# Splitting the row maxima on DVE instead of on POOL, in an attention and feed-forward kernel

## Time and profile before

| | |
|---|---|
| three runs | median 218.69 us (218.49 to 219.09) |
| profiled execution | 218.52 us, span 216.7 us |
| PE, matrix products | busy 166.3 us, 77% |
| DVE | 151.9 us, 70%, 287 instructions |
| ACT | 141.2 us, 65%, 286 instructions |
| POOL | 105.1 us, 49%, 275 instructions |
| mean granted clock of PE | 0.952 |

### The profile page before, as it was taken

The page is one execution under the profiler, slowest core; times in us unless marked ns, Lnnn a source line. Parts: engine busy times, 40 slices in busy tenths (PEclk is TensorE's granted clock), DMA queues, the critical chain, the costliest instruction groups (busy, mean ns, idle before and its releaser), DMA issues.

```text
span 216.7 us, 4308 instructions
## 1 busy us (share of the span) xinstructions
PE 166.3 (77%) x1378; PEld 97.9 (45%) x1378; DVE 151.9 (70%) x287; ACT 141.2 (65%) x286; POOL 105.1 (49%) x275
## 2 busy tenths in 40 slices
PE   0008629674969896899899899989989987974963
PEld 0003214332757553475466467556556644523412
DVE  2549906443597976768997998898899796156382
ACT  3220136983657887577888778779688877973531
POOL 4403242419863829772653565284264456345250
PEclk9999999975899999589999999999999999999799
DMA  4945589671112721162025006104300000000000
GB/s 146 321 141 157 149 257 367 255 214 31 28 46 64 207 54 48 49 200 76 0 73 152 27 22 182 51 0 137 113 0 5 0 28 8 20 5 0 27 0 24
DMA packets 15714, 19.95 MB, mean 92 GB/s; under 512 B 2604, under 2 KB 14012, under 8 KB 14684
## 3 DMA queue, kind: packets, MB, share of 16 engines
q1 hardware_dynamic: 11753, 14.94, 23.4%
q10 hardware_dynamic: 3939, 4.74, 6.6%
HBM read 15.20 MB, written 4.19 MB: 90 GB/s over the span
## 4 chain that ended last, share of the span: by engine, by line
PE 38%; POOL 20%; issue 12%; DVE 11%; DMA 9%; ACT 5%; ACTq 1%; SPq 1%; POOLq 0%; DVEq 0%
PE psO L462 9%; PE psA L428 8%; PE psB L446 6%; POOL hw L332 6%; DMA q_stack<-mt 5%; DVE mneg L761 3%; PE psG L564 3%; PE psG L534 2%; PE psG L554 2%; POOL hrms L989 2%; DVE h L851 2%; DMA q_stack<-q_scratch 2%; DMA q_scratch<-q_parts 2%; DVE gu L840 2%; ACT th L682 2%
## 5 line engine op out<-in xcount | busy, mean ns | idle before, releaser
L761 DVE TENSOR_REDUCE mneg<-psA 128x2 f32<-128x512 f32 x128 | 81.8, 678 | 22.1 <-PE psA L428 22.1
L608 ACT ACTIVATE probs<-psB 128x512 f32<-128x512 f32 x128 | 73.2, 597 | 12.3 <-PE psB L446 11.8
L428 PE MATMUL psA<-k_stack,q_stack 72*128 72x256 bf16 x256 | 54.3, 303 | 16.9 <-DMA q_stack<-q_scratch 16.9
L446 PE MATMUL psB<-q_stack,k_stack 75*128 75x256 bf16 x256 | 51.4, 285 | 9.1 <-DMA q_stack<-mt 7.1
L462 PE MATMUL psO<-probs,vt 128*32 128x256 f32 x512 | 37.7, 416 | 1.0 <-ACT probs L608 1.0
L428 PEld LDWEIGHTS psA<-k_stack,q_stack 72*128 72x128 bf16 x256 | 22.9, 104 | 34.0 <-issue 25.5
L332 POOL TENSOR_TENSOR hw<-h,lnw 128x512 f32<-128x512 f32 x15 | 19.1, 1274 | 34.9 <-DVE h L851 26.5
L446 PEld LDWEIGHTS psB<-q_stack,k_stack 75*128 75x128 bf16 x256 | 24.2, 102 | 21.6 <-DMA q_stack<-mt 7.9
L462 PEld LDWEIGHTS psO<-probs,vt 128*32 128x32 f32 x512 | 14.1, 115 | 15.2 <-issue 7.9
L840 DVE SCALAR_TENSOR_TENSOR gu<-th,psG 128x512 f32<-128x512 f32 x15 | 10.3, 687 | 9.3 <-ACT th L682 9.3
L682 ACT ACTIVATE th<-psG,tscale 128x512 f32<-128x512 f32 x15 | 10.3, 688 | 8.0 <-PE psG L534 8.0
(11 more groups left out here) (133 smaller groups left out, 261.6 us busy)
## 6 DMA issues: line engine op xcount, KB each, us to landing
k_stack<-k_scratch SPq DMA_DIRECT2D x21, 192.0 KB
q_stack<-q_scratch SPq DMA_DIRECT2D x21, 192.0 KB
q_scratch<-q_parts SPq DMA_DIRECT2D x24, 64.0 KB, 3.1
k_scratch<-k_parts SPq DMA_DIRECT2D x18, 64.0 KB, 3.0
w_sb<-in_L_ffn_w_gate_dram ACTq DMA_DIRECT2D x1, 1024.0 KB, 7.8
w_sb<-in_L_ffn_w_up_dram ACTq DMA_DIRECT2D x1, 1024.0 KB, 10.8
w_sb<-in_L_ffn_w_down_dram ACTq DMA_DIRECT2D x1, 1024.0 KB, 9.0
out_dram<-y_sb SPq DMA_DIRECT2D x8, 128.0 KB, 1.8
```

The lines of the kernel that those rows point to most:

```text
L428: mm = pe.matmul(psA[n % A_BANKS][:, qt * L:(qt + 1) * L], q_stack[0:STACK, t % NBUF, bh, qt * P:(qt + 1) * P], k_stack[0:STACK, t % NBUF, ...
L446: mm = pe.matmul(psB[b % 2][:, lt * L:(lt + 1) * L], k_stack[:, t % NBUF, bh, lt * P:(lt + 1) * P], q_stack[:, t % NBUF, bh, :], start=Tru ...
L608: act.activation(probs[:, b % RING, :], psB[b % 2][:, :], ACT.Exp, scale=SCALE).then_inc(s_exp, 1)
L761: dve.tensor_reduce(mneg[:, k % MBUF, QT * (bh % HALF):QT * (bh % HALF + 1)], psA[n % A_BANKS][:, :].rearrange("p (q l) -> p q l", q=QT), ...
```

## The change

The four operations of the split leave POOL's list and stand in DVE's, at m = 16 + 16 k: behind the last maximum of the half tile and, where h_max has the same m as that maximum, behind h_max. The waits are the same (all 8 maxima of the half tile, and the transpose two half tiles before, for the buffer). Nothing else moves.

```diff
-POOL_M, POOL_RSTD = 21, 71
+DVE_M, POOL_RSTD = 16, 71
...
                                       negate=True).then_inc(s_red, 1)
+                k = half_at(m, DVE_M)
+                if k is not None:
+                    dve.wait_ge(s_red, HALF * (k + 1))
+                    if k >= 2:
+                        dve.wait_ge(s_mt, k - 1)
+                    worst, part = mneg[:, k % MBUF, :], m_parts[:, k % 2]
+                    link(dve.tensor_copy(part[:, 0, :], worst))
+                    link(dve.tensor_tensor(mrest[:, :], worst, part[:, 0, :], ALU.subtract))
+                    link(dve.tensor_copy(part[:, 1, :], mrest[:, :]))
+                    dve.tensor_tensor(part[:, 2, :], mrest[:, :], part[:, 1, :], ALU.subtract).then_inc(s_ms, 1)
                 if m == DVE_W:
...
-                k = half_at(m, POOL_M)
-                if k is not None:
-                    pool.wait_ge(s_red, HALF * (k + 1))
-                    if k >= 2:
-                        pool.wait_ge(s_mt, k - 1)
-                    worst, part = mneg[:, k % MBUF, :], m_parts[:, k % 2]
-                    link(pool.tensor_copy(part[:, 0, :], worst))
-                    link(pool.tensor_tensor(mrest[:, :], worst, part[:, 0, :], ALU.subtract))
-                    link(pool.tensor_copy(part[:, 1, :], mrest[:, :]))
-                    pool.tensor_tensor(part[:, 2, :], mrest[:, :], part[:, 1, :], ALU.subtract).then_inc(s_ms, 1)
```

## The result

The kernel with the split on DVE takes 225.1 us (median of 4 runs, 224.39 to 225.49) against 218.61 before (218.49 to 219.09): ratio 1.0295, 95% interval 1.0269 to 1.032. It is 6.5 us slower; 216.3 was predicted, in a range up to 218.8. On POOL, behind the place that the split left, the old numbers hold again (L996). A ratio leaves out every execution over 1.5% above the fastest one of its kernel, so where executions scatter it can differ from the quotient of the medians, which are of all of them.

A forecast was written before the change was run, and what follows sets the result against it. PE sets the pace in regular tiles, DVE close behind; late splits stopped PE for 7.8 us. Terms -0.4 - 3.9 + 0.8 - 0.5 + 1.7 - 0.1 = -2.4 us took 218.69 to 216.3, range 213.7 to 218.8.

The forecast's parts named there:

- The first split's transpose: At the start, PE transposes at 23.36 instead of 23.76; the gain of 0.4 us goes into the span.
- A split takes 0.72 us of DVE's list: Cost of four linked steps on DVE: 0.68 us, or 0.8 straight behind a maximum.
- The odd-numbered splits: In regular tiles their 0.8 us fall on DVE's 0.44 + 0.34 of waiting and cost nothing.
- One mark of a wrong forecast: Forecast is wrong if ACT or PE waits over 1 us for POOL between 52 and 58 us.
- 4 x 0.43 = 1.7 us lost: Four even-numbered splits in regular tiles (eighth to fourteenth): L795 ends later, so PE's L511 starts 0.43 us later each.
- rival (c): Sixth split: PE idles about 1.5 instead of 2.11 us, its clock stays up, gain up to 2.2, time 214.1; chance 0.18.
- -3.9: Third split: PE's wait near 48 us goes, the first weight transpose (L497) starts 3.7 to 4.2 us earlier, 3.9 taken.
- +0.8: Fourth split: DVE is packed there and PE waits for its result, so 0.8 us is lost.
- POOL's own queue moves up by what the four steps took: Behind the third split, POOL's rests end 1.1 to 2.0 us earlier, just in time for ACT.
- Rival (b): Third split's gain given back by late rests or second weight matrix: 1.3 of 3.9 us remain, time 218.9; chance 0.14.
- -0.1: Sixth split: h_max still waits for POOL's hw, so L511 starts at 88.2 instead of 88.30, gain 0.1 us.
- Rival (a): DVE's and POOL's steps hold each other up at seven places, 5.9 us together, time 222.2, slower; chance 0.12.

The follow-up runs named there:

- fill4: The changed kernel plus four filler products on PE ahead of the transposes of the sixth, eighth, up to the sixteenth split: 219.91 us, ratio 1.0014 to the kernel before.
- second_split: The kernel before, POOL's splits kept, plus the four operations repeated on DVE behind h_max of the sixth, eighth, up to sixteenth half tile, unread: 226.05 us, ratio 1.0272.
- fourth_on_pool: The kernel of fill4 with the fourth split alone back on POOL: 217.79 us, ratio 0.9849 to the kernel before.
- late_even_on_dve: The kernel before with only the sixth, eighth, up to the sixteenth split on DVE, all others on POOL: 225.37 us, ratio 1.0267.
- fourth_on_dve: The kernel before with the fourth split alone moved to DVE: 221.63 us, ratio 1.0137.
- third_on_dve: The kernel before with the third split alone moved to DVE: 219.02 us (215.26 to 222.09), no ratio.
- third_early_pool: The kernel before, all splits on POOL, the third put ahead of the first weight matrix's rounding in POOL's list: 218.76 us, ratio 0.9922.
- odd_on_pool: The changed kernel with every second split, beginning with the second, back on POOL at its old place: 219.2 us, ratio 0.9898 to the kernel before.

## Why the prediction was wrong

**Right.** The first split's transpose comes 23.76 - 16.93 = 6.83 us behind the first product before and 24.25 - 17.77 = 6.48 after: 0.35 earlier, 0.4 was said; but the first B product gained only 0.1 (7.71 us lie between the two, before 7.47), and the tile grew by 0.38. The third split's wait goes and L497 starts at 51.95 (51.0 to 51.5 was said, in a kernel that began 0.84 earlier). A split takes 0.72 us of DVE's list (0.68). The odd-numbered splits are covered, though DVE's wait of 0.34 still stands there (at 140.20) and only the one of 0.44 is gone. A regular tile whose clock stays up grows by 0.49 (0.43); PE's wait of 0.47 lies one product ahead of where it was put, at pass A for its bank and not at L511. L511 at the sixth split starts at 88.34 (88.2). One mark of a wrong forecast was met as well: ACT waited over 1 us for POOL between 52 and 58 (1.20, at 56.49).

**The step that failed first** is "From L511 to the next tile PE has no gap that would take this back; so 4 x 0.43 = 1.7 us lost". It prices a PE that comes 0.43 us late at the full clock. But the delay is idle time of PE, and with it PE fell to the lower clock in two of the four tiles, for 1.5 us more each. The four tiles cost 5.2 us instead of 1.7. The prediction had seen this effect at the sixth split and used it there alone, as a possible gain in rival (c). fill4 and second_split show it from both sides: with PE kept busy no regular tile falls to the lower clock (none of eight in fill4 and fourth_on_pool), and with only DVE's load added they do (two of four, as with the change; one of four in late_even_on_dve).

**The second is the third split**, "-3.9", with the fourth at "+0.8". The gain was there at 51.95 and mostly gone at 66.27. "POOL's own queue moves up by what the four steps took" is the step that failed: it was to be 1.1 to 2.0 us, and it was nothing (7.88 us in place of 7.73 to the end of the rests), since DVE's clipping now met two of POOL's operations, which grew by 1.07 and 0.98 us. Rival (b) named this mechanism, POOL's queue moving up too little, with 2.6 us; in fact 3.1 of 4.4 us were given back by L511. The fourth split took 2.4 us of DVE's list (57.76 to 60.16) in place of 0.8 in this profile, and the clock was at 0.66 from 57 to 66. Together the stretch from 44.70 to 73.19 gained 1.2 us instead of 3.1.

**The third term**, the sixth split, "-0.1": the tile grew by 1.76. Here too PE waits 1.58 and 0.45 in place of 2.11, and the clock was low in both kernels. How much of the 1.76 belongs to the change stays open: the same tile took 22.06, 22.42 and 24.1 us in fourth_on_dve, third_on_dve and third_early_pool, which change nothing in it, and 24.81 in odd_on_pool, whose sixth split is where it was before (all but the first in executions 2 to 3 us above their medians). late_even_on_dve gives 1.98 for it, at the same uncertainty, and second_split 0.08.

**Rival (a)** said 222.2 by DVE and POOL holding each other up, and was nearest in sign and size, for a reason that is seen in one place only. In the regular tiles, for which it was priced, the steps took 0.16 to 0.18 us although h_inv (from 129.66, for 0.32 us) and h_rec (from 130.07, for 0.58) ran beside them. At the fourth split they took 0.49 to 0.68 beside operations of 256 and 2048 elements. The Trainium skill, SBUF — State Buffer, section "SBUF: two separate sides", describes an exclusive lock on ports shared by VectorE and GpSimd; the trace of the fourth split agrees with it (0.68 in place of 0.17 for a copy of 16 elements), and that of the regular tiles shows no hold-up.

**Open.** Why the clock falls in one tile and not in the next with the same waits. The Trainium skill, TensorE: Matmul & The Clock Gate, Part 1, calls the window in which the chip looks at PE's activity free-running, not started by the kernel; by that it is left to chance how a wait lies to the window, which fits the pairs above, but no run here moved a wait step by step to show it. The first two tiles of second_split, which are those of the kernel before, took 53.54 us against 52.10, so nothing below about 1.4 us can be read out of one profile there, and the shares of the third tile and of the fourth split aren't settled. Of the 6.5 us, 5.2 lie in the four regular tiles, where the experiments show the cause: DVE's delay, and the lower clock behind it.

## What to carry to other kernels

Idle time that a change gives to PE in a dense stretch has two prices: the wait itself, and the products behind it at half the clock. Before costing a wait of half a microsecond at half a microsecond, look in the same trace for what PE's products took behind a wait of that kind, and put that case into the range. Price a small operation that moves to another engine by its place in that engine's list, not by its busy share; ask what stands right behind it, and who waits for that. Where a long wait goes, follow the next three or four dependences: here ACT's copies and POOL's rests, on which PE waited 5.5 us later (57.45), took most of the gain.

## What the runs showed of the hardware

Waits of 0.20 and 0.23 us, with 0.22 us between them, were followed by the lower clock in one tile of second_split and not in the one before it; waits of 1.05 and 0.58 likewise in fill4 and fourth_on_pool. Each fall made a tile of 18.65 us 1.4 to 1.7 us longer (20.03 to 20.33). Of the twelve regular tiles with the added steps on DVE behind h_max and no filler (the change, second_split, late_even_on_dve) five fell; of the eight with four products of filler, 0.60 us, ahead of the transpose (fill4, fourth_on_pool) none did.

Dependent DVE operations of 16 elements took 0.16 to 0.18 us at a distance of 0.21; beside POOL's operations of 0.55, 0.67 and 1.97 us the same ones took 0.49 to 0.68, each ending 0.01 to 0.03 us behind POOL's. Beside POOL's operations of one element (0.32 and 0.58 us) they took 0.16 to 0.18. In the other direction, POOL's operations of 256 elements, 0.55 and 0.67 us long, took 1.62 and 1.65 beside DVE's clipping of 1.23 us.
